# One run of scores and transposes per period: the written-out order of a fused decoder kernel

## The reference

```
x = x + attn(layernorm(x))     # 16 heads of width 64, causal, softmax, out product
x = x + xattn(layernorm(x))    # 64 context rows per sequence, mask, softmax
x = x + ffn(layernorm(x))      # silu(x W1) * (x W2), two 1024x1024 gelu layers, x W3

q = einsum('ntc,hdc->nhtd', x_q, w_q)          # the same for k and v
a = einsum('nhtd,nhsd->nhts', q, k) / sqrt(64)
a = softmax(where(t < s, -inf, a))
y = einsum('nhts,nhsd->nthd', a, v)
out = y @ w_o
```

## Time and profile before

| quantity | value |
|---|---|
| median of the runs | 1468.86 us (3 runs, 1468.46 to 1469.24) |
| the profiled execution, its own time | 1471.24 us |
| its span, first to last instruction | 1469.4 us |
| PE busy | 98% of the span |
| DVE / ACT / POOL busy | 85% / 69% / 33% |
| granted PE clock, mean | 0.997 |

### The profile page before, as it was taken

How to read it: one execution, slowest core, us unless ns; L and a number is a source line. 1 busy time by engine, 2 the same in 40 slices (tenths; PEclk the granted TensorE clock), 3 DMA queues, 4 the chain that set the end, 5 groups by cost and what they waited for, 6 DMA issues and landing times.

```text
span 1469.4 us, 29115 instructions
## 1 busy us (share of the span) xinstructions
PE 1446.5 (98%) x10408; PEld 1225.9 (83%) x10408; DVE 1242.6 (85%) x3068; ACT 1020.6 (69%) x2382; POOL 481.7 (33%) x755
## 2 busy tenths in 40 slices
PE   8999999999999999999998899999999999999998
PEld 6888888888888888888887788888888888888887
DVE  7999999999999999999899857788776848888876
ACT  6888888888888888887888754654556445555644
POOL 2545554655556545465444111112111100000000
PEclk9999999999999999999999999999999999999999
DMA  4000100101001010010013435544342593041310
GB/s 159 2 2 2 59 2 16 45 1 59 2 4 56 2 42 18 2 59 1 16 31 101 162 132 189 174 161 148 130 144 94 190 333 117 31 145 59 116 59 31
DMA packets 78277, 113.54 MB, mean 77 GB/s; under 512 B 4768, under 2 KB 54304, under 8 KB 77216
## 3 DMA queue, kind: packets, MB, share of 16 engines
...
...
## 4 chain that ended last, share of the span: by engine, by line
PE 89%; DVE 7%; issue 1%; DMA 1%; ACT 1%; SPq 0%; DVEq 0%
PE bank L1371 11%; PE bank L761 10%; PE bank L681 10%; PE bank L733 8%; PE bank L1215 8%; PE bank L683 8%; PE bank L682 8%; PE bank L1217 7%; PE bank L745 6%; PE bank L1389 4%; PE bank L1341 2%; PE bank L1332 2%; PE bank L1334 2%; PE bank L1330 2%; PE bank L1223 1%
## 5 line engine op out<-in xcount | busy, mean ns | idle before, releaser
L952 POOL TENSOR_SCALAR P<-P,stats 128x512 f32<-128x512 f32 (+3 forms) x512 | 267.3, 541 | 331.4 <-DVE stats L930 331.2
L817 ACT ACTIVATE P<-P,stats 128x384 f32<-128x384 f32 (+3 forms) x512 | 284.1, 560 | 17.3 <-DVE stats L922 17.0
L784 ACT ACTIVATE PT<-bank 128x512 fp32r<-128x512 f32 (+1 forms) x384 | 185.3, 525 | 87.1 <-PE bank L745 85.8
L922 DVE CUSTOM_DVE_ANT_0 P<-bank,cmask 128x384 f32<-128x384 f32 (+3 forms) x512 | 228.4, 483 | 1.2 <-PE bank L733 0.9
L831 DVE TENSOR_TENSOR PT<-bank,PT 128x512 fp32r<-128x512 f32 (+1 forms) x384 | 218.6, 594 | 5.1 <-ACT PT L784 4.1
L1371 PE MATMUL bank<-op,ws 128*128 128x512 f32 x896 | 205.9, 389 | 0.0
L1215 PE MATMUL bank<-Hb,hw 128*128 128x512 f32 x512 | 202.8, 396 | 0.0
L1371 PEld LDWEIGHTS bank<-op,ws 128*128 128x128 f32 x896 | 167.3, 188 | 34.1
L761 PEld LDWEIGHTS bank<-PT,V 128*128 128x128 f32 x1024 | 165.1, 190 | 23.0 <-DVE PT L831 4.3
L761 PE MATMUL bank<-PT,V 128*128 128x512 f32 (+3 forms) x1024 | 176.1, 319 | 3.5 <-DVE PT L831 3.5
L1217 PE MATMUL bank<-Hb,hw 128*128 128x512 f32 x448 | 176.3, 393 | 0.0
...
## 6 DMA issues: line engine op xcount, KB each, us to landing
...
```

The lines of the kernel that those rows point to most:

```text
L784: return e.activation(dst, src, ACT.Copy, scale=scale)
L817: e.activation(p, p, ACT.Exp, bias=st_[:, k:k + 1], scale=-1.0, accum_out=st_[:, 8 + k:9 + k]).then_inc(s_exp, 1)
L922: e.tensor_tensor_reduce(P_tile(P, i, a), banks["S", P, max(i, 1)][a][:, slice(*S_COLS[i])], cmask[:, 512 - n:512], -1.0, 3.0e38, ALU.add, ...
L952: e.tensor_scalar(p, p, stats[P % 4][:, k:k + 1], 1.0, ALU.mult, ALU.mult).then_inc(s_norm, 1)
```

## The change

Only the written-out order changes; each engine has the same items as before, and the program that carries them out is the same. HEAD, BATCH and TAIL are new for PE, ACT, DVE and POOL; SP's list stays. BATCH now is repeated 4 times instead of 6, and HEAD and TAIL are longer for it. The last stretch of TAIL, from about pair 61 on, is as it was.

In the old BATCH a period has two runs of half-array items: T, S, S, T, then `k`, then S and T, then `q` and the rest. In the new one all six stand together as S.3 T.2 S.2 S.1 T T, and `k q v AV AV O` follow (the three of k, q and v in an order that varies). Over all of attention the number of such runs goes from 133 to 95; 37 of the new ones, those of the pairs 12 to 48, are of this form. The six items of a run take twelve banks in turn. The lists of the other engines follow the new order of PE.

```
 BATCH = {
     "PE": """
-        S:0:2 T:-1:0 S:0:1 k:1 T:-1:1 O:-2 AV:-1:0 q:1 AV:-1:1 v:3 T:0:2 S:1:3 S:1:2 T:0:1 k:2 S:1:1 T:0:0 q:2
-        O:-1 AV:0:0 AV:0:1 v:4 T:1:2 S:2:3 S:2:2 T:1:0 k:3 S:2:1 T:1:1 O:0 AV:1:0 q:3 AV:1:1 v:5 T:2:2 S:3:3
-        S:3:2 T:2:0 k:4 S:3:1 T:2:1 q:4 AV:2:0 v:6 AV:2:1 O:1 T:3:2 S:4:3 S:4:2 T:3:0 k:5 T:3:1 S:4:1 q:5 AV:3:0
...
+        k:0 q:0 AV:-2:0 AV:-2:1 v:2 O:-3 S:0:3 T:-1:2 S:0:2 S:0:1 T:-1:0 T:-1:1 k:1 v:3 q:1 AV:-1:0 AV:-1:1
+        O:-2 S:1:3 T:0:2 S:1:2 S:1:1 T:0:0 T:0:1 k:2 q:2 v:4 AV:0:0 AV:0:1 O:-1 S:2:3 T:1:2 S:2:2 S:2:1 T:1:1
+        T:1:0 k:3 v:5 q:3 AV:1:0 AV:1:1 O:0 S:3:3 T:2:2 S:3:2 S:3:1 T:2:1 T:2:0 v:6 k:4 q:4 AV:2:0 AV:2:1 O:1
...
     "DVE": """
-        m:2:0:1 os:0 ql:3 r:2:0 ys:1:1 vl:5 pl:2:2:0 m:3:3:0 m:3:2:1 m:3:2:0 pl:2:2:1 m:3:3:1 pl:2:0:0 pl:2:0:1
-        m:3:1:1 kl:4 ln0:2 m:3:0:0 m:3:1:0 pl:2:1:0 m:3:0:1 pl:2:1:1 r:3:2 ys:2:0 ql:4 r:3:0 ys:2:1 vl:6 os:1
...
+        r:2:2 vl:5 kl:3 ql:3 r:2:0 ys:1:0 ys:1:1 os:0 m:3:3:0 m:3:3:1 pl:2:2:0 pl:2:2:1 m:3:2:0 m:3:1:1
+        m:3:1:0 m:3:0:1 m:3:2:1 pl:2:1:1 m:3:0:0 pl:2:0:0 pl:2:1:0 pl:2:0:1 ln0:2 r:3:2 vl:6 kl:4 ql:4 ys:2:0
+        r:3:0 ys:2:1 os:1 m:4:3:1 m:4:3:0 pl:3:2:1 pl:3:2:0 m:4:0:1 m:4:2:0 m:4:2:1 m:4:1:0 m:4:0:0 m:4:1:1
...
-LOOP = range(6)
+LOOP = range(1, 5)
```

More of the change, by code:

```diff
@@ L29 @@
     "PE": """
[L30 to L34, removed]
+        idle.0 rows.0.0 rows.0.1 idle.1 v.0 k.0 q.0 k.1 v.1 v.2 S.0.3 S.0.2 S.0.1 q.1 v.3 S.1.3 S.1.2 k.2
@@ new lines @@
+        T.0.2 v.4 T.0.1 T.0.0 S.1.1 q.2 k.3 AV.0.0 AV.0.1 S.2.3 T.1.2 S.2.2 q.3 T.1.1 S.2.1 T.1.0 k.4 q.4 v.5
+        S.3.3 S.3.2 AV.1.0 AV.1.1 T.2.0 T.2.2 v.6 v.7 T.2.1 S.3.1 AV.2.0 S.4.3 S.4.2 S.4.1 O.1 AV.2.1 T.3.0
+        T.3.1 T.3.2 O.2 k.5 q.5 AV.3.0 AV.3.1 S.5.3 k.6 S.5.2 S.5.1 T.4.0 T.4.2 q.6 O.3 T.4.1 rows.1.0
+        rows.1.1 S.6.3 S.6.2 AV.4.0 AV.4.1 T.5.2 v.8 k.7 S.6.1 T.5.1 T.5.0 q.7 v.9 O.4 AV.5.0 S.7.3 S.7.2
+        AV.5.1 k.8 S.7.1 T.6.0 T.6.2 q.8 k.9 T.6.1 S.8.3 S.8.2 O.5 AV.6.0 v.10 AV.6.1 S.8.1 T.7.0 T.7.1 T.7.2
@@ L38 @@
[L38 to L42, removed]
@@ L49 @@
[L49 to L53, removed]
@@ L57 @@
+        m.13.1.0""",
     "POOL": """
@@ new lines @@
+    "POOL": """
+        rows_high:1:1 rows_low:1:1 n:-1:3:0 n:-1:3:1 n:-1:2:0 n:-1:2:1 n:-1:0:1 n:-1:0:0 yh:-2 n:-1:1:0
+        n:-1:1:1 n:0:2:1 yl:-2 n:0:2:0 n:0:3:0 n:0:3:1 n:0:0:0 n:0:1:0 n:0:1:1 n:0:0:1 yh:-1 yl:-1 n:1:2:1
+        n:1:3:1 n:1:3:0 n:1:2:0 n:1:0:1 n:1:1:1 yh:0 n:1:0:0 n:1:1:0 yl:0 rs:2 n:2:3:0 n:2:2:1 n:2:2:0 n:2:3:1
+        yh:1 n:2:0:0 n:2:1:1 n:2:0:1 n:2:1:0 yl:1 n:3:3:1 n:3:2:0 n:3:2:1 n:3:0:1 n:3:3:0 n:3:0:0 n:3:1:1
+        n:3:1:0 yh:2 yl:2 n:4:3:0 n:4:3:1 n:4:2:0 n:4:2:1 yh:3 n:4:0:0 n:4:1:0 n:4:0:1 n:4:1:1 yl:3 n:5:2:0
+        n:5:3:1 n:5:3:0 n:5:2:1 yh:4 n:5:1:0 n:5:0:0 n:5:0:1 n:5:1:1 yl:4 n:6:2:0 n:6:2:1 n:6:3:1 n:6:3:0
+        n:6:0:1 n:6:1:0 n:6:1:1 n:6:0:0 yh:5 yl:5 rows_high:2:0 rows_low:2:0""",
@@ new lines @@
+        u.0.2 g.0.3 u.0.3 g.0.4 u.0.4 g.0.5 u.0.5 g.0.6 u.0.6 g.0.7 u.0.7 ft.3""",
+    "ACT": """
+        ph.44.0.1 ph.44.1.0 ph.44.1.1 ph.44.0.0 e.45.2.1 e.45.1.1 e.45.2.0 e.45.0.1 e.45.0.0 kh.46 yo.44.0
+        qh.46 yo.44.1 e.45.1.0 vh.48 ph.45.2.1 ph.45.2.0 e.46.3.1 e.46.3.0 ph.45.0.1 ph.45.1.0 ph.45.1.1
+        e.46.0.0 ph.45.0.0 kh.47 e.46.2.1 e.46.2.0 vh.49 e.46.1.1 qh.47 e.46.0.1 e.46.1.0 yo.45.0 yo.45.1
+        ph.46.2.1 ph.46.2.0 e.47.3.1 ph.46.0.1 ph.46.1.1 ph.46.0.0 ph.46.1.0 kh.48 e.47.2.0 e.47.3.0 e.47.0.1
+        e.47.2.1 qh.48 e.47.0.0 e.47.1.0 yo.46.0 vh.50 yo.46.1 e.47.1.1 ph.47.2.1 ph.47.2.0 e.48.3.1 ph.47.0.0
+        e.48.3.0 ph.47.0.1 e.48.2.0 ph.47.1.0 e.48.0.0 kh.49 ph.47.1.1 e.48.2.1 e.48.0.1 e.48.1.1 yo.47.0
+        qh.49 vh.51 e.48.1.0 yo.47.1 ph.48.2.0 ph.48.2.1 ph.48.0.0 e.49.2.1 e.49.3.1 ph.48.1.1 e.49.3.0
+        ph.48.0.1 ph.48.1.0 e.49.2.0 kh.50 e.49.1.1 e.49.1.0 qh.50 yo.48.0 e.49.0.0 vh.52 e.49.0.1 yo.48.1
+        ph.49.2.0 ph.49.2.1 ph.49.0.1 ph.49.1.1 ph.49.1.0 kh.51 e.50.3.0 ph.49.0.0 e.50.3.1 vh.53 qh.51
+        e.50.2.1 e.50.2.0 e.50.0.0 e.50.1.1 e.50.1.0 e.50.0.1 yo.49.0 e.51.3.0 e.51.1.0 vh.54 yo.49.1 e.51.0.1
+        ph.50.1.0 ph.50.0.0 ph.50.1.1 ph.50.0.1 ph.50.2.1 kh.52 ph.50.2.0 e.51.2.0 qh.52 e.51.0.0 e.51.2.1
+        e.51.3.1 yo.50.0 e.51.1.1 e.52.3.0 e.52.2.1 yo.50.1 e.52.0.1 e.52.0.0 e.52.3.1 kh.53 ph.51.0.0
+        e.52.2.0 ph.51.2.0 ph.51.1.0 ph.51.0.1 ph.51.2.1 e.52.1.0 qh.53 ph.51.1.1 e.52.1.1 vh.55 yo.51.0
+        e.53.3.0 e.53.1.0 ph.52.2.0 yo.51.1 ph.52.1.0 ph.52.0.1 ph.52.0.0 ph.52.1.1 ph.52.2.1 e.53.2.0 kh.54
+        e.53.3.1 e.53.1.1 e.53.2.1 e.53.0.1 qh.54 e.53.0.0 yo.52.0 kh.55 yo.52.1 vh.56 e.54.3.1 ph.53.2.1
+        ph.53.2.0 e.54.3.0 ph.53.0.1 ph.53.1.0 e.54.0.0 ph.53.1.1 e.54.2.0 qh.55 ph.53.0.0 kh.56 e.54.2.1
+        e.54.1.1 e.54.1.0 e.54.0.1 vh.57 e.55.2.1 yo.53.0 e.55.2.0 yo.53.1 e.55.3.1 ph.54.2.0 ph.54.0.0
+        ph.54.0.1 ph.54.2.1 qh.56 e.55.3.0 e.55.1.1 kh.57 e.55.0.0 e.55.0.1 ph.54.1.1 e.55.1.0 ph.54.1.0
+        yo.54.0 e.56.3.0 yo.54.1 ph.55.1.0 ph.55.1.1 ph.55.2.0 ph.55.2.1 ph.55.0.0 e.56.0.0 ph.55.0.1 e.56.3.1
+        e.56.2.0 e.56.2.1 e.56.1.1 vh.58 qh.57 e.56.0.1 vh.59 e.56.1.0 yo.55.0 yo.55.1 ph.56.2.1 ph.56.2.0
+        vh.60 ph.56.0.1 ph.56.0.0 e.57.3.0 e.57.3.1 ph.56.1.0 e.57.2.1 kh.58 e.57.0.0 qh.58 e.57.2.0 ph.56.1.1
+        yo.56.0 e.57.1.0 e.57.1.1 e.57.0.1 e.58.3.1 e.58.2.1 e.58.2.0 yo.56.1 ph.57.2.1 ph.57.2.0 ph.57.1.0
+        ph.57.0.0 e.58.3.0 ph.57.0.1 ph.57.1.1 kh.59 vh.61 e.58.1.1 e.58.0.0 e.58.1.0 qh.59 yo.57.0 e.58.0.1
+        yo.57.1 e.59.2.1 ph.58.2.0 ph.58.2.1 e.59.3.1 e.59.3.0 kh.60 vh.62 ph.58.0.1 ph.58.0.0 ph.58.1.0
+        ph.58.1.1 e.59.2.0 vh.63 qh.60 e.59.0.1 yo.58.0 e.59.1.0 e.59.1.1 e.59.0.0 e.60.3.0 e.60.2.0 e.60.3.1
+        e.60.2.1 yo.58.1 e.60.1.0 kh.61 ph.59.0.0 ph.59.0.1 ph.59.2.1 ph.59.2.0 e.60.0.1 qh.61 ph.59.1.1
+        e.60.1.1 ph.59.1.0 e.60.0.0 yo.59.0 e.61.3.0 e.61.2.0 e.61.1.1 ph.60.2.1 ph.60.2.0 e.61.3.1 e.61.0.1
+        yo.59.1 kh.62 ph.60.0.1 ph.60.0.0 ph.60.1.0 ph.60.1.1 e.61.2.1 xth.0.0.0 qh.62 e.61.0.0 yo.60.0
+        e.61.1.0 yo.60.1 xth.0.0.1 ph.61.2.1 ph.61.2.0 ph.61.0.0 fh.0 e.62.3.0 e.62.3.1 fh.1 ph.61.1.1
+        e.62.0.0 e.62.2.1 ph.61.0.1 kh.63 e.62.2.0 fh.2 qh.63 e.62.1.1 yo.61.0 fh.3 e.62.1.0 ph.61.1.0
+        e.62.0.1 bqh xkh.0 fh.4 yo.61.1 xkh.1 ph.62.2.0 ph.62.2.1 fh.5 fh.6 e.63.2.1 e.63.3.1 xfh.0 e.63.2.0
+        e.63.3.0 xfh.1 ph.62.1.1 ph.62.1.0 ph.62.0.0 ph.62.0.1 e.63.1.0 e.63.1.1 big.5 e.63.0.0 xvh.0 xcc
+        e.63.0.1 xvh.1 big.6 yo.62.0 xe.0 yo.62.1 ph.63.0.0 ph.63.2.1 xph.0 ph.63.0.1 ph.63.1.0 ph.63.1.1
+        ph.63.2.0 fh.7 fh.8 big.7 yo.63.0 fh.9 yo.63.1 big.8 xvh.2 fh.10 xvh.3 xth.0.1.0 xth.0.1.1 big.9 fh.11
+        big.10 silu.0.0 silu.0.1 big.11 silu.0.2 hh.0.1 silu.0.3 hh.0.3 silu.0.4 fh.12 silu.0.5 fh.13 fh.14
+        big.12 hh.0.5 silu.0.6 silu.0.7 fh.15 hh.0.6 hh.0.7 fh.16 big.13 big.14""",
@@ new lines @@
+    "POOL": """
+        rows_high.6.1 rows_low.6.1 n.45.3.0 n.45.3.1 n.45.2.0 n.45.2.1 n.45.0.1 n.45.0.0 yh.44 n.45.1.0
+        n.45.1.1 n.46.2.1 yl.44 n.46.2.0 n.46.3.0 n.46.3.1 n.46.0.0 n.46.1.1 n.46.1.0 n.46.0.1 yh.45 yl.45
+        n.47.2.1 n.47.3.1 n.47.3.0 n.47.2.0 n.47.0.1 n.47.1.1 n.47.0.0 n.47.1.0 yh.46 yl.46 rs.7 n.48.3.0
+        n.48.2.1 n.48.2.0 n.48.3.1 n.48.0.0 yh.47 n.48.1.0 n.48.0.1 yl.47 n.48.1.1 n.49.2.0 n.49.3.1 n.49.3.0
+        n.49.2.1 n.49.0.1 n.49.1.0 n.49.0.0 yh.48 n.49.1.1 yl.48 n.50.2.0 n.50.3.0 n.50.2.1 n.50.3.1 n.50.0.0
+        n.50.0.1 n.50.1.0 n.50.1.1 yh.49 yl.49 n.51.2.0 n.51.2.1 n.51.3.0 n.51.3.1 n.51.0.1 n.51.1.0 n.51.0.0
+        n.51.1.1 yh.50 yl.50 rows_high.7.0 n.52.3.1 rows_low.7.0 n.52.2.0 n.52.0.1 n.52.2.1 rows_high.7.1
+        n.52.3.0 n.52.0.0 n.52.1.0 n.52.1.1 yh.51 yl.51 rows_low.7.1 n.53.3.1 n.53.3.0 n.53.0.1 n.53.2.1
+        n.53.1.0 n.53.2.0 lpow.0.0 yh.52 yl.52 n.53.1.1 n.53.0.0 n.54.3.1 n.54.2.1 n.54.2.0 n.54.1.0 n.54.0.0
+        n.54.1.1 n.54.3.0 yh.53 yl.53 n.54.0.1 n.55.3.0 n.55.0.0 n.55.1.1 n.55.2.0 n.55.1.0 n.55.2.1 n.55.3.1
+        n.55.0.1 yh.54 yl.54 n.56.3.0 n.56.2.0 n.56.3.1 n.56.2.1 n.56.1.0 n.56.1.1 n.56.0.0 n.56.0.1 yh.55
+        yl.55 n.57.3.0 n.57.3.1 n.57.2.1 n.57.2.0 n.57.1.0 n.57.1.1 n.57.0.1 n.57.0.0 n.58.3.1 yh.56 yl.56
+        n.58.2.1 n.58.2.0 n.58.3.0 n.58.1.1 n.58.0.1 n.58.0.0 n.58.1.0 yh.57 yl.57 n.59.3.0 n.59.3.1 n.59.1.1
+        n.59.2.1 n.59.2.0 n.59.1.0 n.59.0.0 n.59.0.1 n.60.3.0 yh.58 n.60.2.1 yl.58 n.60.3.1 n.60.2.0 n.60.1.1
+        n.60.0.0 n.60.1.0 n.60.0.1 yh.59 yl.59 n.61.3.1 n.61.2.0 n.61.2.1 n.61.3.0 n.61.0.0 n.61.0.1 n.61.1.1
+        n.61.1.0 yh.60 yl.60 n.62.2.1 n.62.3.0 n.62.2.0 n.62.3.1 n.62.0.1 n.62.1.0 n.62.0.0 n.62.1.1 yh.61
+        yl.61 n.63.2.1 pz n.63.3.1 n.63.3.0 n.63.2.0 n.63.1.1 n.63.0.1 n.63.0.0 n.63.1.0 yh.62 yl.62 lpow.0.1
+        yh.63 yl.63 hh.0.0 hh.0.2 hh.0.4 lpow.1.0""",
```

248 lines of the change are left out of this document (140 added, 108 removed).

## The result

| quantity | before | after |
|---|---|---|
| median of the runs | 1468.55 us (20 runs) | 1471.60 us (20 runs) |
| ratio, 95% interval | | 1.0021 [1.0014, 1.0027] |
| profiled execution: own time, span | 1471.24, 1469.4 us | 1471.21, 1469.4 us |
| S.0.3 to S.12.3 | 139.05 | 139.32 |
| S.12.3 to S.46.3 (34 periods) | 409.68 (12.05 each) | 408.97 (12.03 each) |

The account below looks back on a forecast made before the run. PE's own stream was taken to bound attention. Of 0.43 us saved per period, bank waits take 0.30; 36 periods gain 4.7 us, HEAD and TAIL 0.7: 5.4 off 1468.86 gives 1463.5 us, forecast's own range 1460 to 1466.5.

Parts of the forecast that it names:

- The loss at the banks: Attention periods: PE's run waits for DVE to read PSUM banks, costing 0.30 us of the 0.43 us saved per period.
- Steps saved: PE's stream in attention: fewer changes between half-array and full items shorten a period from 12.05 to 11.62 us, 0.43 less.
- The start of the fifth item and the order of events: In a run, counted from S.3: two maxima, then two copies; number five starts at 2.37 us, number six at 3.04.
- Loss: 0.28 us in every one of the periods: In a run, number six starts at 3.04 us, when DVE's copies free its banks, not at 2.76.
- The 0.02 that I had put on the bank of S.2: First full item after a run: waiting for the maximum that reads a bank of S.2 costs 0.02 us per period on average.
- HEAD and TAIL: ... leave about 0.7: Outside the 36 periods: two runs less save 0.9 us; bank waits and DVE's lead in the hand-over leave about 0.7.
- No wait for banks: Rival for attention runs: DVE's readers are in time, the steps saved stand whole, 1452.5 us; chance 0.14.
- DVE paces the period: Rival for attention: DVE's work plus its remaining waits keep the period at 12.05 us, time 1468.9 us; chance 0.18.
- AV waits for its copies: Rival for attention: copies reach AV late; slower from 0.13 us of wait per period, 1474.3 us at 0.3; chance 0.10.

## Why the prediction was wrong

Two steps failed. The loss at the banks was mis-sized, by little per period but by most of a small net gain, and the part outside the steady periods, put at a gain of 0.7 us without a walk of DVE's list, became a loss of 4.

- **Steps saved (right).** 11.62 us for a period without waits; 11.69 measured once the first readings are short. The full items took 8.28 to 8.29 us where I had 8.26. In the run my split was off and its sum right: S.2 takes 0.60 us and S.1 0.65 there, where I had 0.53 and 0.72.
- **The start of the fifth item and the order of events (right).** First maximum at 1.01, release at 2.32, copies' end at 2.99, all as walked from the earlier trace rows. The mechanism of the forecast, PE behind DVE's four readings, is what binds.
- **"Loss: 0.28 us in every one of the periods" (the term that failed, by its size).** The run took 3.74 us instead of 3.66. Of the difference 0.05 is the wait after the release: I took 0.05 from one row, and for the sixth item it is 0.10 in the mean. Another 0.05 lies between the sixth item and the first full one, 0.65 instead of 0.60: with short first readings these transposes take 0.59 us in the 21 periods in which the sixth item does not wait, and 0.64 to 0.69 in all periods in which it waits, in either kernel. The 0.02 that I had put on the bank of S.2 is not seen. With 0.03 in the full items the period is 12.03, not 11.92. It sounds small, but the forecast's gain was itself a difference of 0.43 and 0.30: 0.11 us took 3.7 us of the 4.4 that I expected from S.12.3 to S.46.3.
- **"HEAD and TAIL: ... leave about 0.7" (failed).** The forecast has a gain of 1.0 us outside S.12.3 to S.46.3: these 0.7 and two more steady periods. I counted steps there and did not walk DVE's list. S.46.3 to the second block got 4.0 us longer, and S.0.3 to S.12.3 0.3 longer. Together with the missing gain of 1.0 this is the larger part, 5.3 us, of the 8.9 us between forecast and trace. In the tail the run of six is there at first, but what DVE has to do ahead of it is not that of a steady period, and with the old order behind S.48.3 the loss is gone (222.37 us against 222.41 before).
- **The rivals.** *No wait for banks* is excluded in the whole computation; with short readings its period nearly stands. *DVE paces the period* had the right time for the steady part and the wrong cause. The page "TensorEngine Tiling (Array Packing)" of the Trainium skill, section "PSUM Bottleneck", says that tiling speeds up the products but not the copies out of PSUM. It points at the right engine here, but the bound is four readings in a row and not DVE's total (92% busy, and 0.46 us less of work per period left the period at 12.03 us). *AV waits for its copies* did not occur in the steady periods: the change is slower, but not by this. The slower outcome that did occur, a tail with a late DVE, was no rival of mine.
